# Second attention: a third bank for the score maxima, and the turned maxima and outputs moved into the projection banks

## What is computed

```
q = xn @ wq.T + bq ; k = xn @ wk.T + bk ; v = xn @ wv.T + bv      # 16 heads of 16
scores = einsum('bhsd,bhtd->bhst', q, k) / sqrt(16)
attn = softmax(scores, axis=-1)                                   # over all 512 keys
out  = einsum('bhst,bhtd->bhsd', attn, v) @ wo.T + bo
x    = x + out * silu(ffn)
```

## Time and profile before

| what | value |
|---|---|
| runs | 1984.23, 1987.37, 1990.66 us; median 1987.37 |
| the profiled execution's own time | 1987.64 us |
| its span in the profile | 1985.8 us |
| TensorE busy | 1847.7 us (93%) |
| VectorE busy | 1411.8 us (71%) |
| ScalarE busy | 1191.2 us (60%) |
| `score`, line 1463 | 512, mean 465 ns |
| `score_t`, line 1472 | 512, mean 406 ns |
| `maximum`, line 1584 | 512, mean 686 ns |
| `exps`, line 1677 | 512, mean 599 ns |

### The profile page before, as it was taken

One profiled execution on the slowest core, in us unless ns is written; L12 is line 12 of the kernel. 1 busy time (PEld: TensorE's weight loads), 2 busy tenths in 40 slices (PEclk: granted clock), 3 DMA queues, 4 the chain that ended last, 5 costly groups with the idle time before them and its releaser, 6 DMA issues. The chain is left out here.

```text
span 1985.8 us, 32448 instructions
## 1 busy us (share of the span) xinstructions
PE 1847.7 (93%) x11568; PEld 1411.5 (71%) x11568; DVE 1411.8 (71%) x2881; ACT 1191.2 (60%) x2809; POOL 605.4 (30%) x958
## 2 busy tenths in 40 slices
PE   1999999999999999999999959998799999999997
PEld 1887888878778888878888758887455555555553
DVE  5785885885885867858858854443677777777773
ACT  3665675674664765756756755554466666666664
POOL 0354353443543443543534523222100110011012
PEclk9999999999999999999999989999799999999999
DMA  6111111211111111111101157332733444353421
GB/s 234 42 34 33 44 43 27 49 44 33 43 33 44 41 25 46 41 33 43 44 25 41 43 170 286 120 115 74 202 106 101 133 146 120 112 163 93 132 70 43
DMA packets 104047, 162.34 MB, mean 82 GB/s; under 512 B 11984, under 2 KB 53456, under 8 KB 103376
## 3 DMA queue, kind: packets, MB, share of 16 engines
q1 hardware_dynamic: 103368, 159.75, 28.1%
q10 hardware_dynamic: 520, 0.52, 0.1%
HBM read 80.55 MB, written 46.14 MB: 64 GB/s over the span
## 5 line engine op out<-in xcount | busy, mean ns | idle before, releaser
L1584 DVE TENSOR_REDUCE nm<-ps 128x1 f32<-128x512 f32 x512 | 338.4, 686 | 120.3 <-PE ps L1463 117.6
L1677 ACT ACTIVATE pt<-pst 128x512 f32<-128x512 f32 x512 | 290.2, 599 | 194.1 <-PE pst L1472 191.6
L805 POOL TENSOR_SCALAR pr<-pr,rinv 128x128 f32<-128x128 f32 (+3 forms) x512 | 263.2, 533 | 374.8 <-DVE rinv L693 374.8
L573 ACT ACTIVATE pr<-sc,nmax 128x128 f32<-128x128 f32 (+3 forms) x512 | 268.1, 527 | 143.4 <-DVE nmax L682 141.9
L682 DVE TENSOR_REDUCE nmax<-sc 128x1 f32<-128x128 f32 (+3 forms) x512 | 223.3, 485 | 76.5 <-PE sc L409 76.4
L1463 PE MATMUL ps<-kb,qb 96*128 96x512 f32 x512 | 237.1, 465 | 27.5 <-DMA kb<-z_scratch 15.3
L811 POOL TENSOR_TENSOR qk<-ra,rb 128x256 f32<-128x256 f32 x256 | 182.9, 735 | 206.4 <-DVE rb L704 170.9
L1463 PEld LDWEIGHTS ps<-kb,qb 96*128 96x128 f32 x512 | 97.9, 191 | 185.5 <-DVE nm L1584 123.6
L1472 PE MATMUL pst<-qb,kb 128*128 128x512 f32 x512 | 207.0, 406 | 3.4 <-ACT pt L1677 2.9
L421 PE MATMUL w<-ident,pr 128*128 128x128 f32 x1280 | 170.6, 280 | 25.7 <-DVE rb L704 19.8
L1419 POOL TENSOR_TENSOR so<-so,g_sb 128x256 f32<-128x256 f32 x32 | 23.5, 733 | 535.4 <-DVE so L1621 535.4
(11 more groups left out here) (213 smaller groups left out, 4227.6 us busy)
## 6 DMA issues: line engine op xcount, KB each, us to landing
k<-k SPq DMA_DIRECT2D x256, 128.0 KB, 2.2
z_scratch<-zt SPq DMA_DIRECT2D x96, 256.0 KB, 2.5
qb<-z_scratch SPq DMA_DIRECT2D x64, 192.0 KB, 3.8
kb<-z_scratch SPq DMA_DIRECT2D x64, 192.0 KB, 4.0
raw<-in_w SPq DMA_DIRECT2D x16, 640.0 KB, 6.1
raw<-in_w SPq DMA_DIRECT2D x8, 704.0 KB, 4.2
xa<-in_x SPq DMA_DIRECT2D x2, 2048.0 KB, 13.8
x<-in_x SPq DMA_DIRECT2D x8, 512.0 KB, 4.0
```

The lines of the kernel that those rows point to most:

```text
L573: act.activation(pr[:, h, SOFF[i]:SOFF[i] + (i + 1) * P], sc[:, bank, at:at + (i + 1) * P], ACT.Exp, bias=nmax[:, h, i:i + 1], accum_out=r ...
L805: pool.tensor_scalar(p, p, rinv[:, h, i:i + 1], 1.0, ALU.mult, ALU.mult).then_inc(scaled, 1)
L1584: dve.tensor_reduce(nm[:, g % 2, i, h:h + 1], ps[:, i % 2, :], AXX, ALU.max, negate=True).then_inc(max_done, 1)
L1677: act.activation(pt[:, g % 2, h, i, :], pst[:, i % 2, :], ACT.Exp).then_inc(exp_done, 1)
```

## The change

`ps` gets a third bank, and a score now waits for the maximum three before it: bank n % 3 in place of i % 2, and `max_done` at n - 1 in place of n. The bank comes from `pn`, which is gone. `turn_o` writes bank 0 of `w`; `turn_n` writes bank 0, or bank 1 for group 2 (`NBANK`). Each of these turns now waits for the last reader of its bank; and three users of `w` behind them wait for the readers of the turns. The copies read `w`.

```diff
--- before.py
+++ after.py
@@ -1291,10 +1291,9 @@
         on = t.sb("on", [P, NT, C])
         ot_hi, ot_lo = (t.sb(n, [P, NC, T], F32R) for n in ("ot_hi", "ot_lo"))
         so = t.sb("so1", [P, 2, C])
-        ps = t.ps("ps", [P, 2, 512])
+        ps = t.ps("ps", [P, 3, 512])
         pst = t.ps("pst", [P, 2, 512])
         po = t.ps("po1", [P, 512])
-        pn = t.ps("pn", [P, 512])
         w = t.ps("w1a", [P, 2, 512])
         sn_hi_done = t.sem("a_sn_hi_done")
         xs_in = [t.sem(f"a_xs_in{r}") for r in range(2)]
@@ -1333,6 +1332,8 @@
 
 
 
+        NBANK = (0, 0, 1, 0)
+
         Z_PE, Z_ACT, Z_DVE = ((0, 2), (2, 0)), ((0, 3), (2, 1)), ((1, 1), (2, 2))
         V_PE, V_DVE = ((1, 0), (1, 3), (2, 1), (2, 3)), ((1, 1), (2, 0), (2, 2), (3, 0))
         O_PE, O_DVE = ((0, 2), (1, 1), (2, 0), (2, 3)), ((0, 3), (1, 2), (2, 1), (3, 0))
@@ -1444,6 +1445,8 @@
                 def project_v(b, i):
                     if i > 1:
                         pe.wait_ge(vn_done, NT * b + i - 1)
+                        if i == 2 and b > 1:
+                            pe.wait_ge(on_done, NG1 * (b - 1))
                     elif b > 0:
                         pe.wait_ge(c.zt_lo_done, 4 * b + i + 1)
                     else:
@@ -1459,8 +1462,9 @@
                     if h == 0 and i == 0:
                         pe.wait_ge(stack_in[g], 64 * (q // NG1) + 64)
                     n = 16 * q + 4 * h + i
-                    pe.wait_ge(max_done, n)
-                    pe.matmul(ps[:, i % 2, :], qb[0:2 * S3, g, h // 2, i * P:(i + 1) * P], kb[0:2 * S3, g, h, :],
+                    if n > 2:
+                        pe.wait_ge(max_done, n - 1)
+                    pe.matmul(ps[:, n % 3, :], qb[0:2 * S3, g, h // 2, i * P:(i + 1) * P], kb[0:2 * S3, g, h, :],
                               start=True, stop=True).then_inc(s_done, 1)
 
                 def score_t(q, g, h, i):
@@ -1485,19 +1489,40 @@
                         mm.then_inc(av_done, 1)
 
                 def turn_n(q):
+                    b, g = q // NG1, q % NG1
                     pe.wait_ge(sn_done, q + 1)
-                    if not isinstance(q, int) or q > 3:
+                    if q > 3:
                         pe.wait_ge(on_done, q - 2)
-                    for i in range(NT):
-                        mm = pe.transpose(pn[:, i * P:(i + 1) * P], sn[:, i].rearrange("p a b -> p (a b)").bitcast(F32), c.ident[:])
+
+                    if g == 2 and b < B - 1:
+                        pe.wait_ge(vn_done, NT * (b + 1) + NT)
+                    elif g == 2:
+                        pe.wait_ge(so_done, NT * (b - 2) + NT)
+                    elif q == 0:
+                        pe.wait_ge(c.zt_lo_done, 3)
+                    elif g == 0 and b > 1:
+                        pe.wait_ge(so_done, NT * (b - 2) + 3)
+                    elif g % 2 and b < B - 1:
+                        pe.wait_ge(c.zt_lo_done, 2 * (2 * (b + 1) + g // 2) + 1)
+                    for i in range(NT):
+                        mm = pe.transpose(w[:, NBANK[g], i * P:(i + 1) * P], sn[:, i].rearrange("p a b -> p (a b)").bitcast(F32), c.ident[:])
                     mm.then_inc(n_turned, 1)
 
                 def turn_o(q, n_turns):
+                    b, g = (q + 2) // NG1, (q + 2) % NG1
                     pe.wait_ge(ou_done, q + 1)
                     pe.wait_ge(n_dve, n_turns)
                     pe.wait_ge(n_act, n_turns)
-                    for i in range(NT):
-                        mm = pe.transpose(pn[:, i * P:(i + 1) * P], ou[:, i * P:(i + 1) * P], c.ident[:])
+                    if b < B - 1 and g % 2 == 0:
+                        pe.wait_ge(c.zt_lo_done, 2 * (2 * (b + 1) + g // 2) + 1)
+                    elif b < B - 1 and g == 1:
+                        pe.wait_ge(vn_done, NT * (b + 1) + 1)
+                    elif b == B:
+                        pe.wait_ge(so_done, NT * (B - 2) + 3)
+                    elif g == 3 and b > 0:
+                        pe.wait_ge(so_done, NT * (b - 1) + 1)
+                    for i in range(NT):
+                        mm = pe.transpose(w[:, 0, i * P:(i + 1) * P], ou[:, i * P:(i + 1) * P], c.ident[:])
                     mm.then_inc(o_turned, 1)
 
                 def turn_on(b, k):
@@ -1507,6 +1532,9 @@
                         pe.wait_ge(vn_done, NT * (b + 2) + NT // 2 + k + 1)
                     else:
                         pe.wait_ge(so_done, NT * (b - 1) + NT // 2 + k + 1)
+                    if k == 1 and b < B - 1:
+                        pe.wait_ge(n_dve, NG1 * b + NG1 + 3)
+                        pe.wait_ge(n_act, NG1 * b + NG1 + 3)
                     for i in range(NT):
                         mm = pe.transpose(w[:, k, i * P:(i + 1) * P], on[:, i, k * P:(k + 1) * P], c.ident[:])
                     mm.then_inc(on_turned, 1)
@@ -1518,6 +1546,8 @@
                             pe.wait_ge(c.zt_lo_done, 4 * (b + 2) + 2 + i + 1)
                     else:
                         pe.wait_ge(so_done, NT * b + i - 1)
+                        if i == 2 and b < B - 1:
+                            pe.wait_ge(on_done, NG1 * (b + 1) + 2)
                     for k in range(NC):
                         oh, ol = (a[:, k, i * P:(i + 1) * P] for a in (ot_hi, ot_lo))
                         pe.matmul(w[:, i % 2, 0:C], oh, wo_hi[:, k, :], start=(k == 0), stop=False)
@@ -1580,8 +1610,9 @@
                 def maximum(q, g, h, i):
                     if h == 0 and i == 0 and not (isinstance(q, int) and q < 2):
                         dve.wait_ge(sn_done, q - 1)
-                    dve.wait_ge(s_done, 16 * q + 4 * h + i + 1)
-                    dve.tensor_reduce(nm[:, g % 2, i, h:h + 1], ps[:, i % 2, :], AXX, ALU.max, negate=True).then_inc(max_done, 1)
+                    n = 16 * q + 4 * h + i
+                    dve.wait_ge(s_done, n + 1)
+                    dve.tensor_reduce(nm[:, g % 2, i, h:h + 1], ps[:, n % 3, :], AXX, ALU.max, negate=True).then_inc(max_done, 1)
 
                 def split_n(q, g):
 
@@ -1594,12 +1625,12 @@
 
                 def take_n(q, g):
                     dve.wait_ge(n_turned, q + 1)
-                    dve.tensor_copy(qb[2 * S3:P, g, 0, :], pn[0:2 * D1, :]).then_inc(n_dve, 1)
+                    dve.tensor_copy(qb[2 * S3:P, g, 0, :], w[0:2 * D1, NBANK[g], :]).then_inc(n_dve, 1)
 
                 def take_o(q, g):
 
                     dve.wait_ge(o_turned, q + 1)
-                    v = pn[:].rearrange("p (t h d) -> p t h d", t=NT, h=HG)
+                    v = w[:, 0, :].rearrange("p (t h d) -> p t h d", t=NT, h=HG)
                     dve.reciprocal(inv[:], v[:, :, :, D1:D1 + 1]).then_inc(inv_done, 1)
                     dve.wait_ge(inv_done, q + 1)
                     dve.tensor_tensor(on[:, :, g * HG * D1:(g + 1) * HG * D1].rearrange("p t (h d) -> p t h d", h=HG),
@@ -1678,7 +1709,7 @@
 
                 def take_n(q, g):
                     act.wait_ge(n_turned, q + 1)
-                    act.copy(qb[2 * S3:P, g, 1, :], pn[2 * D1:4 * D1, :]).then_inc(n_act, 1)
+                    act.copy(qb[2 * S3:P, g, 1, :], w[2 * D1:4 * D1, NBANK[g], :]).then_inc(n_act, 1)
 
                 def take_o(q):
                     act.wait_ge(av_done, q + 1)
```

## The result

| | before | after |
|---|---|---|
| median of 20 runs | 1988.57 us | **1994.41 us** |
| lowest to highest | 1984.23 to 1990.76 | 1990.30 to 2000.23 |
| ratio | | **1.0031, 95% interval [1.0025, 1.0037]** |
| profiled execution, its span | 1987.64, 1985.8 | 1996.72, 1994.9 |

The change costs 5.8 us. The profiled execution of after lies 2.3 over its own median and that of before 0.9 under its own, so the two traces are 9.1 apart; 7.8 of that lie in the second attention.

What follows compares the result with a forecast made beforehand. TensorE was taken to set the pace, so only its waits count. Middle batches +8.3, prologue -0.4, batch 0 -0.9, batch 7 -1.2 gave +5.8, cut to +5.3 for rounding: 1992.9 us from the profiled 1987.64, range 1987 to 1998.

Steps and rivals of the forecast that it cites:

- The third bank gains 0.10 of 0.34: Second to third turned score in a plain quarter: step falls from 0.82 to 0.72 us, held by ScalarE's exponential.
- Fourth quarters: Last four slots (h,0) to (h,3) of a group: -0.21 us each in groups 0 and 2, -0.44 in group 3.
- The four stalls: Moved turns wait for VectorE: turn_o +0.75 us in groups 0 and 2, +0.64 in group 1; turn_n +0.70 in group 1.
- Middle batches: Batches 1 to 6 of the second attention: stalls minus bank gains, +1.38 us a batch, +8.3 in all.
- Batch 0: First batch, whose first group has no weighing: gain, -0.9 us together, bounds 0 and -2.8.
- batch 7: Last batch, no projections so no new wait, 12 quarters at 0.10: -1.2 us, bounds -0.6 and -2.
- Prologue: Start of the second attention, where VectorE sets the pace: a score further ahead gives about -0.4 us, bounds 0 and -1.
- The waits costed at nothing: Other new waits (so_done, n_dve, n_act, on_done, zt_lo_done before turn_n): work ends a quarter or more earlier, 0 us.
- Rival 1: Exponentials do not hold the third turned score, each plain exchange gives 0.35 us: 1980.9 us, chance 0.06.
- Rival 2: VectorE's maximum behind each of 26 stalls is 0.43 us late and this carries on, 11 us more: 2004, chance 0.07.
- Rival 3: Wait on ScalarE takes back all 0.34 us of the third bank, only the turns' cost stays: 2006 us, chance 0.04.
- Rival 4: New stalls let TensorE's clock fall, one fall a batch costing 2 us, six of them 12: 2005 us, chance 0.03.

Runs made afterwards that it cites:

- half exponentials: Exponentials of 256 of the 512 columns, rest of pt set to 1: on the changed kernel 1979.19 us, on the kernel before 1981.22 us.
- e6: The changed kernel with the late wait of each turn put first in its list of waits: 1993.18 us, ratio 1.0031 to the kernel before.
- turns only: The changed kernel with the scores back on two banks, turns still moved to the projection banks: 2007.86 us, ratio 1.0103 to the kernel before.

## Why the forecast was right, and by what it missed

The forecast, 1992.9, lies 1.5 below the measured 1994.41, and the reasons held. Set against the medians of 20 runs the loss was 5.8 where 5.5 was forecast, and that closeness is in part luck: 5.3 was summed up for the second attention, the two traces differ there by 7.8, and the 2.5 between is made of the misses below. The prediction also held that a loss of 6 us could hardly be told from none. With 20 runs of each kernel it can: the interval is 1.0025 to 1.0037. By the steps of the sum:

- **The third bank gains 0.10 of 0.34.** Measured 0.08 to 0.11 in each of the six quarters. That ScalarE's latency sets it was argued from the earlier trace rows; the half exponentials show it for five of them. The third quarter of group 1 had only 0.10 to lose, as the prediction says (0.57 to 0.47).
- **Fourth quarters.** -0.21 forecast, -0.25 and -0.23 measured. In group 3 -0.44 forecast, -0.45 measured: there the turned scores do follow by 0.47, as the timeline of after has it:

```profile
1699.24 0.40 PE L1476 MATMUL pst<-qb,kb 128*128 128x512 f32 x1
1699.48 0.40 PE L1467 MATMUL ps<-kb,qb 96*128 96x512 f32 x1
1699.71 0.39 PE L1476 MATMUL pst<-qb,kb 128*128 128x512 f32 x1
```

- **The four stalls: right in place, small in size.** Forecast 0.75, 0.64, 0.75, 0.70; measured 0.81, 0.70, 0.80, 0.75, so 0.22 a batch more. This is the term that was mis-sized: "what does such a wait add beyond the end? 0.12". The row for it, is of a turn whose late wait stands first. The new waits stand last. With the late wait first (`e6`) the middle batch comes back to the forecast's 1.38, so the order is the cause; the single quarters of batch 3 in that run lie within 0.03 of the forecast. The other kind, `turn_n` behind the last `take_v`, in the timeline of after:

```profile
1662.77 0.41 DVE L1643 TENSOR_TENSOR vn<-w1a,bv 128x256 f32<-128x256 f32 x1
...
1663.30 0.42 PEld L1508 LDWEIGHTS w1a<-ident,sn 128*128 128x128 f32 x4 [0.97 <-issue]
```

  End at 1663.18, load 0.12 behind it.
- **Middle batches** +8.3 forecast, +9.5 measured. **Batch 0** -0.9 and -1.5, **batch 7** -1.2 and -1.3. **Prologue** -0.4 and +0.4, and the tail 0 and +0.7. Over all profiles the prologue lay between 21.4 and 23.1 us with no relation to the edit, so a sign can't be read from it. The 0.5 taken off for rounding was not there.
- **The waits costed at nothing** cost nothing: no other wait on the readers of `w` shows, and every quarter without one of the four late turns is at most 0.03 longer than before. By group, the sum's own terms give +1.24 for group 1 and -0.64 for group 3, and +1.36 and -0.65 were measured; the 1.1 in the prediction's list of signs does not fit its sum.
- **Rival 1** (ScalarE keeps up) fell with the step of 0.71. With it falls the prediction's reading of the rule on rotating banks in the Trainium skill (Perfetto Trace Analysis, Optimizing Tensor Performance) as a forecast of size. So read it gave 0.34, and here it was 0.10; with short exponentials the reading comes near, 0.30 to 0.33.
- **Rival 2** (lateness carried on) fell, though the slack was not where the prediction had it. The maximum behind a stall waits 0.45 for its score (1675.22 above; 0.43 was forecast). The 0.97 of the earlier trace rows stands ahead of that place; behind it, at the first maximum of the next quarter, VectorE had no idle time before, and waits 0.35 for TensorE after:

```profile
1671.01 0.69 DVE L1584 TENSOR_REDUCE nm<-ps 128x1 f32<-128x512 f32 x1
```

```profile
1676.89 0.69 DVE L1615 TENSOR_REDUCE nm<-ps 128x1 f32<-128x512 f32 x1 [0.35 <-PE ps L1467]
```

  The stall held TensorE's next score back more than VectorE, so nothing is carried on: the quarter after a stall is not longer than before (-0.09, -0.08, -0.11, -0.01).
- **Rival 3** (the bank gives nothing) fell with turns only. **Rival 4** (the clock) did not come: 1.00 in every 4 us between 1460 and 1944, holes of 0.7 and all.

What stays open: the prologue's spread, and 1.3 us between the two profiles that lie ahead of the second attention, in code that is the same. Over the ten profiles the first score lay between 1396.3 and 1401.0, so 1.3 is within that spread.

## What to carry to other kernels

Before adding a bank, look for the next wait on the same chain and read its bare step somewhere in the trace where nothing else holds it: the gain is the difference of the two steps (0.82 to 0.72), not the wait in the list (106.8 us, of which the bank returned 14). When the bank is paid for by sharing, what decides is which reader's result the newcomer stands behind: the same sharing with older readers turned 5.8 us lost into 8.7 gained. And where several waits stand ahead of one instruction, write the late one first: here that was worth 0.2 us a batch in the trace, too little to tell in the total time.

## What was not expected of the hardware

A late wait costs more when it stands last in the list than when it stands first: the load starts 0.11 to 0.12 after the releasing instruction's end against 0.05 to 0.06, the product 0.15 against 0.06. Places between were not tried. The list of waits shows such a load as held by "issue" (18.4 us of line 1525 above), not by VectorE, so the engine that is waited for can't be read from that row; the row of the product behind it still names VectorE. The Trainium skill (Perfetto Trace Analysis, Identifying Dependency Chains) says that an instruction with waits on several engines may have separate semaphore instructions inserted ahead of it; the rows fit that, with a price of about 0.06 us to the load. No row shows such an instruction itself.
